# The fill of attention: fillers of the whole array with 512 columns instead of 256 in the other half of the rows

## What is computed

```
qkv = x @ qkv_w + qkv_b
scores = einsum('bhnqd,bhnkd->bhnqk', qb, kb) * scale      # block n against blocks n-1 and n
attn = softmax(where(allowed, scores, NEG))
out = einsum('bhnqk,bhnkd->bhnqd', attn, vb)
mixed = gate * local + (1 - gate) * remote_h
x = x + layernorm(mixed @ out_w + out_b)
x = x + layernorm(ffn(layernorm(x)))
```

## Time and profile before

| what | us |
|---|---|
| median of 3 runs | 560.15 (558.89 to 562.59) |
| the profiled execution, its own time | 559.23 |
| its span, from first to last instruction | 557.4 |
| TensorE busy | 506.9 (91%) |
| VectorE busy | 424.0 (76%) |
| ScalarE busy | 298.3 (54%) |
| GpSimd busy | 338.8 (61%) |

### The profile page before, as it was taken

The page is one execution under the profiler, slowest core; times in us unless marked ns, Lnnn a source line. Parts: engine busy times, 40 slices in busy tenths (PEclk is TensorE's granted clock), DMA queues, the critical chain, the costliest instruction groups (busy, mean ns, idle before and its releaser), DMA issues. The chain is left out here.

```text
span 557.4 us, 16662 instructions
## 1 busy us (share of the span) xinstructions
PE 506.9 (91%) x5277; PEld 312.7 (56%) x5280; DVE 424.0 (76%) x1954; ACT 298.3 (54%) x820; POOL 338.8 (61%) x799
## 2 busy tenths in 40 slices
PE   8878679999999999999999998869999999999991
PEld 3434324556556665555555665535677677577671
DVE  5986696988888888998899887645647777675655
ACT  2665305888888888888888888713212211211110
POOL 4799202688888888688888889960122343333241
PEclk9999855999999999999999999989999999999997
DMA  4466450332112332123331100000000000000001
GB/s 128 137 214 176 150 98 2 101 92 69 49 27 59 81 63 64 38 41 63 62 64 40 27 4 4 4 1 1 0 1 1 20 19 0 19 20 0 20 19 38
DMA packets 49058, 28.09 MB, mean 50 GB/s; under 512 B 6808, under 2 KB 48056, under 8 KB 48976
## 3 DMA queue, kind: packets, MB, share of 16 engines
q1 hardware_dynamic: 47648, 26.73, 19.0%
q10 hardware_dynamic: 1328, 0.36, 0.3%
HBM read 17.90 MB, written 8.91 MB: 48 GB/s over the span
## 5 line engine op out<-in xcount | busy, mean ns | idle before, releaser
L1096 DVE CUSTOM_DVE_ANT_0 added<-psS,maskq 128x256 bf16<-128x256 f32 x512 | 200.5, 414 | 34.8 <-PE psS L937 21.9
L1316 ACT ACTIVATE probs<-psST 128x512 f32<-128x512 f32 x240 | 143.2, 597 | 43.2 <-PE psST L973 41.7
L973 PE MATMUL psST<-qst,kst 50*128 50x128 bf16 x992 | 101.0, 222 | 0.0
L937 PE MATMUL psS<-kst,qst 48*128 48x256 bf16 x448 | 91.5, 286 | 2.4 <-DVE rowmax L1096 1.3
L994 PE MATMUL psPV<-probs,vst 128*10 128x128 f32 x1984 | 79.9, 277 | 11.9 <-POOL probs L1231 8.1
L1760 ACT ACTIVATE hT<-fpsH 128x512 f32<-128x512 f32 x32 | 19.1, 597 | 121.7 <-PE fpsH L1504 121.7
L1228 POOL TENSOR_SCALAR_AFFINE_SELECT probs<-probs 128x256 f32<-128x256 f32 x150 | 61.7, 412 | 4.3 <-ACT probs L1316 4.1
L1231 POOL TENSOR_SCALAR_AFFINE_SELECT probs<-probs 128x256 f32<-128x256 f32 x150 | 61.2, 408 | 0.0
L937 PEld LDWEIGHTS psS<-kst,qst 48*128 48x128 bf16 x448 | 25.2, 95 | 62.6 <-issue 36.3
L994 PEld LDWEIGHTS psPV<-probs,vst 128*10 128x10 f32 x1984 | 43.9, 91 | 27.1 <-issue 16.6
L973 PEld LDWEIGHTS psST<-qst,kst 50*128 50x128 bf16 x992 | 55.8, 95 | 0.0
(11 more groups left out here) (198 smaller groups left out, 1092.5 us busy)
## 6 DMA issues: line engine op xcount, KB each, us to landing
q_parts<-early SPq DMA_DIRECT2D x8, 384.0 KB, 2.6
k_parts<-early SPq DMA_DIRECT2D x8, 384.0 KB, 2.7
qst<-q_parts SPq DMA_DIRECT2D x32, 96.0 KB
kst<-k_parts SPq DMA_DIRECT2D x32, 96.0 KB
X<-in_L_attn_x_dram SPq DMA_DIRECT2D x8, 256.0 KB, 3.3
qst<-q_parts SPq DMA_DIRECT2D x32, 64.0 KB
kst<-k_parts SPq DMA_DIRECT2D x32, 64.0 KB
out_dram<-res SPq DMA_DIRECT2D x8, 256.0 KB, 2.3
```

The lines of the kernel that those rows point to most:

```text
L937: last = nc.tensor.matmul(bank[:, a], q, kst[rows, slot, ring(n - 1, 2)], start=True, stop=True)
L973: last = nc.tensor.matmul(bank[:, a, side * P:(side + 1) * P], kst[rows, slot, ring(n - 1 + side)], qst[rows, slot, ring(n)], start=not ma ...
L1096: taken = nc.vector.tensor_tensor_reduce(added[:, 2 * (g % 2) + a], psS[g % 2][:, a], mask, 1.0, NEG * 4, ALU.add, ALU.max, rowmax[:, n.mo ...
L1316: nc.scalar.activation(probs[:, g ^ 1], psST[g % 2][:].rearrange("p a c -> p (a c)"), ACT.Exp, scale=SCALE).then_inc(s_exp.sem, 1)
```

## The change

In the fill the filler behind each score is no longer a product of 64 rows and 256 columns in the half that the score leaves free, but a product of `keep_warm`: all 128 rows and 512 columns, once per score. The bank is as before, psA or psC in turn. The call in the drain (L1019) stays as it was.

```diff
--- before.py
+++ after.py
@@ -1013,7 +1013,7 @@
                         if (s + 2).live:
                             score(s + 2, g, a)
                             if not s.live:
-                                beside((psA, psC)[(g + 1) % 2], (g + 1) % 2, 2 * P)
+                                keep_warm(nc, (psA, psC)[(g + 1) % 2][:], filler, 1)
                         if s.live:
                             if not (s + 2).live:
                                 beside(psS[g % 2][:].rearrange("p a k -> p (a k)"), g % 2, 2 * P)
```

## The result

The changed kernel took 573.25 us (median of four runs, 571.59 to 576.98), the kernel before in the same comparison 561.31: a ratio of 1.023, with a 95% interval of 1.016 to 1.030. Slower was forecast, with 575 us and a range of 559 to 579. Its profiled execution has a span of 572.8 us, 15.4 more than before, and its own time is 574.59.

What follows compares the result with a forecast made beforehand. The fill was taken as bound by a DVE-PE loop at the low clock; PE would become its bound, 16 units of 1.79 us against 12.68 in all. 559.23 + 15.9 = 575.1, so 575 us, range 559 to 579.

Steps and rivals of the forecast that it cites:

- The fillers stand in line: In the fill, whole-array fillers can't lie beside a score: four pieces a unit run in line instead of two.
- The price of a unit: A fill unit, two scores and two fillers with shape changes: 1.79 us at low clock, 1.02 at full.
- the way from a score to a whole-array product: In a fill unit, score start to whole-array product: 0.35 us at low clock, 0.137 of it no streaming.
- The clock stays low: TensorE's clock stays at one half through the fill and rises in step 1 as before; chance 0.60.
- rival A: Clock rises within the fill; 560.0 to 564.3 us for rises after 3.0 to 13 us; chance 0.31.
- What a rise gives back: A clock rise in the fill saves 4.1 us in steps 0 and 1 and the next interval, 3.3 at least.
- Rival B: Fill's shape changes hidden, 1.28 us a low-clock unit: 556.5 with a rise (chance 0.06), 567 at low clock (0.02).
- Rival C: The change does nothing, since step 0 waits anyway for loads or the maxima brought by DMA; chance 0.01.
- All delay reaches the end: Every us of delay at 81.08, where the fill ends and step 0 begins, passes to the kernel's end.

Runs made afterwards that it cites:

- fill_half512: Kernel before with its fill fillers widened to 512 columns, still in the half of the rows the score leaves free; ratio to before 1.001.
- fill_full256: Changed kernel with its whole-array fill fillers cut from 512 to 256 columns; ratio to the kernel before 1.017.
- fill_grouped: Changed kernel with both whole-array fillers of a unit behind its second score, two changes of shape instead of four; 567.6 us, ratio to before 1.016.
- fill_full32: Changed kernel with its whole-array fill fillers cut from 512 to 32 columns; ratio to the kernel before 1.001.
- head_full: Changed kernel plus 8 whole-array fillers at the head of attention's TensorE program; median 561.46 us, ratio to the kernel before 1.001.
- fill_dense: Changed kernel with six whole-array fillers behind each fill unit's second score instead of one behind each score; 570.2 us, ratio to before 1.016.
- head_half: Kernel before, its half-array fill kept, plus 8 whole-array fillers at the head of attention; median 557.34 us, ratio to before 0.996.
- head_one: Kernel before plus 8 whole-array fillers at attention's head, its fill fillers replaced by one whole-array filler per unit; 559.2 us, ratio 0.998.
- head_hold: Kernel before plus 8 whole-array fillers at attention's head; old fill fillers replaced by one whole-array filler behind each unit of fill and step 0; ratio 0.996.
- head_bridge: head_hold plus seven whole-array fillers behind step 0's first mask product, where PE waited for the maxima's DMA; 555.19 us, ratio to the kernel before 0.991.

## Why the prediction was right

- **The fillers stand in line.** Right. The timeline shows it, and fill_half512 shows the reverse: the same columns beside the scores cost 1.1 us.
- **The price of a unit.** 1.79 us was forecast at the low clock, 1.73 measured; 1.02 forecast at the full clock, 1.07 measured. The term that was mis-sized is the way from a score to a whole-array product: 0.137 over streaming was read from a single pair in step 0, and in the fill it is 0.11. Over 32 ways that is 0.8 us of the forecast 15.9. fill_full256, fill_grouped and fill_full32 took this price apart into columns and changes of shape; each fill came within 0.3 us of what was expected from 1.73.
- **The clock stays low.** Right, at a chance of 0.60, and with a comparison for a reason; that it came out so is in part luck. I argued that the new fill is nearer to step 0's mix than to a row of fillers. The runs bear out the comparison, not a reason: two whole-array fillers a unit, alternating or grouped, left the clock at 0.50 over 24 to 27 us, six raised it in 3.0. Activity alone didn't raise it, which rival A had on its side: PE was busy for 26.52 of 27.47 us, and the clock stayed low. Still rival A was near: the same fill, entered with the clock up (head_full), keeps it up, and the change then costs 4.1 us instead of 11.9.
- **What a rise gives back.** Too small: 4.1 us forecast, 5.7 measured in fill_dense. I had taken step 16 as the model of step 0 at the full clock; its interval of 7.63 holds work of steps 15 and 14 that step 0 hasn't (6.76; DVE has 42 instructions in the one and 35 in the other). It didn't enter the forecast, only the prices of the rivals.
- **Rival B**, changes of shape hidden: false by fill_full32, and by the unit of 1.73 us, where hidden changes gave 1.28. **Rival C**, a step 0 that waits anyway: false, its mark was 14.48 us late. A wait for the maxima's DMA does stand there once the fill is short: 0.9 to 1.4 us in head_half (1.1), head_one and head_hold.
- **All delay reaches the end.** Right: 14.48 us at three marks in a row. The 0.9 us more is in the low clock around the entry of the feed-forward. The measured medians are 11.9 us apart, less than the 15.4 of the two spans; the profiled execution of before (559.23) was faster than its median (561.31), that of the change (574.59) slower (573.25). So 575 lies nearer to the measured 573.25 than my terms do: from the median of before the same 15.9 us would have given 577.2.

Not settled: which pauses in step 0 let the clock fall. It fell in head_full after one of 0.65 us (a wait for DVE), in head_one after one of 0.86 and in head_hold at the end of one of 1.44 (both the DMA); it held in fill_dense, which has no filler in step 0 either, with one of 0.26. Only head_hold and head_bridge differ by the pause alone. The execution's chance has a part in it: of the 12 runs of head_hold, three took 552 to 553 us at a mean clock of 0.987 to 0.990, the others 558 to 564 at 0.965 to 0.978; and of those of head_full one took 556.5 at 0.990, the others 560.5 to 566 at 0.966 to 0.980.

## What to carry to other kernels

A filler is free only where the array's rows are: beside a product on half of the rows, in the other half, 256 columns cost nothing (512 cost 1.1 us over the fill), and on the whole array a filler cost its columns and two changes of shape. Here score and filler took 0.87 us at the low clock, against 0.4. Before adding filler work at a low clock, look for the idle stretch that let the clock fall; 8 fillers there, with one whole-array filler a unit behind them, kept the fill at the full clock, where 32 in the fill alone could not raise it. And when a stretch gets shorter, look for what arrives next: here a small DMA, whose wait let the clock fall again until it was bridged too.

## What I had not expected of the hardware

- A busy PE is not a clock that rises. In fill_full256 PE is busy for 20.95 of 20.95 us by its records, at 0.50 throughout; that busy time holds the changes of shape too.
- Going up and staying up are different. Whole-array fillers one at a time between scores did not raise the clock in 27 us (changed kernel) and did hold it for 17 (head_full); one per unit held it for the 11.3 us of the fill (head_one), and the half-array fillers for 5.6 (head_half).
- More work can be as cheap as less: 96 whole-array fillers in the fill took 29.1 us, 32 took 27.5, because the 96 raised the clock.
- A change between half-array and whole-array products costs 0.10 to 0.12 us at the low clock and some 0.1 at the full one, even for a product of 32 columns. "TensorE: Matmul & The Clock Gate" of the Trainium skill, Part 2, step 1, says that TensorE pulls a weight load ahead of running products when the row groups don't conflict or when the load goes to the background weight buffer. The trace of fill_grouped agrees where the shape stays: both loads of its two fillers are over 0.13 us after 82.50. Where the shape changes nothing of that is seen (82.20, 0.32 us from a score of 0.213 to its filler's load). No record says which buffer a load goes to, so the rows show where the rule's case ends and not why; the price goes by the measurement.
